# A transformer block on one core: first layer norm applied to a host-turned copy of the input, its moments spread over partitions through DRAM

## The reference, cut to what matters

```python
B, L, C = 32, 256, 288; H = 16; D = 18; FF = 1152; EPS = 1e-6
def _layernorm(x):
    mu = mean(x, -1); var = mean((x - mu)**2, -1)
    return (x - mu) * rsqrt(var + EPS)
ada = silu(c) @ W_ada + b_ada
shift_msa, scale_msa, gate_msa, shift_mlp, scale_mlp, gate_mlp = split(ada, 6)
h = _layernorm(x) * (1 + scale_msa) + shift_msa
x = x + gate_msa * attention(h, W_qkv, b_qkv, W_proj, b_proj)   # 16 heads of 18 channels
h = _layernorm(x) * (1 + scale_mlp) + shift_mlp
x = x + gate_mlp * (gelu(h @ W_fc1 + b_fc1) @ W_fc2 + b_fc2)
```

## Time and profile before

| what | value |
|---|---|
| median of 3 runs | 1234.8 us |
| the profiled execution's own time | 1228.32 us |
| span of its profile | 1226.5 us |
| PE, TensorE matmuls | 1181.1 us busy (96%), 9863 instructions |
| DVE, VectorE | 901.8 us (74%) |
| ACT, ScalarE | 866.1 us (71%) |
| POOL, GpSimd | 540.3 us (44%) |
| DMA | 188.91 MB, queue q1 busy 48.3% of 16 engines |

### The profile page before, as it was taken

The page is one execution under the profiler, slowest core; times in us unless marked ns, Lnnn a source line. Parts: engine busy times, 40 slices in busy tenths (PEclk is TensorE's granted clock), DMA queues, the critical chain, the costliest instruction groups (busy, mean ns, idle before and its releaser), DMA issues.

```text
span 1226.5 us, 27564 instructions
## 1 busy us (share of the span) xinstructions
PE 1181.1 (96%) x9863; PEld 1064.3 (87%) x9863; DVE 901.8 (74%) x1928; ACT 866.1 (71%) x1485; POOL 540.3 (44%) x557
## 2 busy tenths in 40 slices
PE   6888999999999999999999999999999999999977
PEld 5666999999998999999999999999999999997777
DVE  5687777877777787778777777777777787775553
ACT  5387777777777777777777777777777777778721
POOL 3012544444454444445454444444444445443364
PEclk9799999999999999999999999999999999999999
DMA  8554555554555554445555444555554555444220
GB/s 265 171 169 138 167 167 164 164 154 144 163 160 159 168 166 145 157 157 162 167 166 164 147 159 150 166 165 167 161 153 148 158 166 159 162 149 140 87 68 20
DMA packets 134330, 188.91 MB, mean 154 GB/s; under 512 B 24544, under 2 KB 102422, under 8 KB 133947
## 3 DMA queue, kind: packets, MB, share of 16 engines
q1 hardware_dynamic: 134033, 186.71, 48.3%
q10 hardware_dynamic: 162, 0.44, 0.1%
HBM read 121.92 MB, written 64.63 MB: 152 GB/s over the span
## 4 chain that ended last, share of the span: by engine, by line
PE 84%; SPq 5%; DMA 4%; DVE 3%; ACT 2%; issue 1%; POOL 0%; ACTq 0%; POOLq 0%; DVEq 0%
PE a_bank L867 10%; PE x_bank L785 10%; PE score_bank L808 9%; PE turn_bank L834 9%; PE st_bank L822 9%; PE b_bank L867 8%; PE b_bank L881 6%; PE b_bank L882 5%; PE b_bank L883 5%; PE a_bank L848 4%; PE x_bank L793 4%; SPq L623 2%; DMA qk_rows<-qst 1%; DMA ql<-zeros 1%; PE x_bank L759 1%
## 5 line engine op out<-in xcount | busy, mean ns | idle before, releaser
L1138 DVE TENSOR_REDUCE mx<-score_bank 128x2 f32<-128x512 f32 x512 | 342.0, 687 | 95.8 <-PE score_bank L808 93.7
L953 ACT ACTIVATE e<-st_bank 128x1024 f32<-128x1024 f32 x256 | 262.4, 1025 | 125.8 <-PE st_bank L822 123.5
L1287 POOL TENSOR_TENSOR gl<-gl_raw,gh 128x512 fp32r<-128x512 f32 (+1 forms) x160 | 194.3, 1221 | 226.4 <-DVE gh L1203 226.4
L946 ACT CAST ql<-mxt 4x256 fp32r<-4x256 f32 x512 | 206.2, 403 | 7.4 <-DVE mxt L1147 0.6
L808 PEld LDWEIGHTS score_bank<-kl,ql 122*128 122x128 f32 x1024 | 146.9, 190 | 42.0 <-issue 24.4
L808 PE MATMUL score_bank<-kl,ql 122*128 122x256 f32 x1024 | 174.6, 293 | 5.6 <-DMA ql<-zeros 3.3
L881 PE MATMUL b_bank<-w,gh 128*128 128x288 f32 x576 | 174.5, 303 | 2.2 <-DVE tmp L1209 1.9
L822 PE MATMUL st_bank<-ql,kl 122*128 122x512 f32 x512 | 165.7, 405 | 7.7 <-ACT e L953 6.9
L882 PE MATMUL b_bank<-w,gh 128*128 128x288 f32 x576 | 170.5, 296 | 0.0
L883 PE MATMUL b_bank<-w,gl 128*128 128x288 f32 x576 | 170.3, 296 | 0.0
L834 PE MATMUL turn_bank<-e,ve 128*32 128x256 f32 x2048 | 123.8, 382 | 0.3 <-ACT e L953 0.3
(11 more groups left out here) (152 smaller groups left out, 2473.1 us busy)
## 6 DMA issues: line engine op xcount, KB each, us to landing
qk_rows<-qst SPq DMA_DIRECT2D x128, 256.0 KB, 5.3
ql<-qk_rows SPq DMA_DIRECT2D x384, 72.0 KB
kl<-qk_rows SPq DMA_DIRECT2D x378, 72.0 KB
o_rows<-on SPq DMA_DIRECT2D x128, 128.0 KB
gate<-gates SPq DMA_DIRECT2D x32, 432.0 KB, 4.4
xin<-in_x SPq DMA_DIRECT2D x32, 288.0 KB, 5.9
x<-in_x SPq DMA_DIRECT2D x32, 288.0 KB, 3.0
out<-x SPq DMA_DIRECT2D x32, 288.0 KB, 4.5
```

The costliest lines, as they stand in the source:

```text
L946: last = nc.scalar.copy(rows[:, :, :, t, a, :], src)
L953: nc.scalar.activation(e[:, j % 4, :, :, :].rearrange("p u i l -> p (u i l)"), st_bank[:, :, :, :].rearrange("p u i l -> p (u i l)"), ACT. ...
L1138: nc.vector.tensor_reduce(mx[:, j // HP, i, :, col:col + 1], score_bank[i][:, :].rearrange("p (t l) -> p t l", t=NT), AX.X, ALU.max).then_ ...
L1287: nc.gpsimd.tensor_tensor(gl[:, cols], g[:, cols], gh[:, cols].bitcast(F32), ALU.subtract).then_inc(g_lo, 1)
```

## The change

The host hands over a second copy of x, `x_turned`, with channels on the partitions: per sample [128, 3, 256], the third block being the last 32 channels four times. The normalisation is made on that copy. For this the mean and the reciprocal deviation of every token must be present on every partition: VectorE and GpSimd put them in `mr1` (128 partitions x 2 tokens x 2 numbers), a DMA writes them to DRAM (`m_rows`, 2 KB a sample), and a second DMA reads these 2 KB back to all 128 partitions (`mrow`). Two `tensor_tensor` instructions over 128x768 then subtract the mean and multiply by the reciprocal deviation, in place in `xt_in`. ACT reads `xt_in` where it read `x_bank`. PE's `xt` is gone. `xin` has one buffer instead of two.

All five orders are written anew, head and tail too; the steps are those of before without PE's `xt`, and with `xc`, `mw`, `mr` on SyncE and `mod1` on POOL. In the head, ScalarE issues the first sample's `m_rows` write and read, x[0] is fetched ahead of the conditioning weights, and the conditioning products `mod` stand ahead of the first `s`.

```diff
 PE_ORDER = [
+    ("st", 0, 0), ("fc1", -3, 4), ("s", 0, 5), ("v", 1, 1), ("fc2", -3, 0), ("proj", -2, 0), ("s", 0, 6),
+    ("st", 0, 1), ("fc2", -3, 1), ("proj", -2, 1), ("st", 0, 2), ("s", 0, 7), ("fc2", -3, 2), ("st", 0, 3),
+    ("qk", 2, 0), ("fc2", -3, 3), ("s", 1, 0), ("pv", 0, 0), ("fc2", -3, 4), ("st", 0, 4), ("s", 1, 1),
...
 SYNC_ORDER = [
+    ("rr", -2, 0), ("qkr", 0, 10), ("qkr", 0, 11), ("qkr", 0, 12), ("or", -2, 0), ("or", -2, 1), ("xc", 2, 0),
...
+    ("rr", -2, 3), ("qkr", 0, 21), ("mw", 2, 0), ("qkw", 1, 0), ("sr", -1, 0), ("qkr", 0, 22), ("qkr", 0, 23),
+    ("or", -2, 5), ("qkr", 0, 24), ("qkr", 0, 25), ("mr", 2, 0), ("qkw", 1, 1), ("ln1_stats", 3, 0), ("rr", -2, 4),
...
 PE_HEAD = [
+    ("qk", 0, 0), ("qk", 0, 1), ("qk", 0, 2), ("gate5", 0, 0), ("v", 0, 0), ("gate2", 0, 0), ("v", 0, 1),
+    ("gate5", 0, 1), ("mod", 0, 0), ("s", 0, 0), ("gate5", 0, 2), ("s", 0, 1), ("gate2", 0, 1), ("gate2", 0, 2),
+    ("s", 0, 2), ("qk", 1, 0), ("s", 0, 3), ("qk", 1, 1), ("s", 0, 4), ("qk", 1, 2), ("s", 0, 5), ("st", 0, 0),
...
 ACT_HEAD = [
+    ("xt", 0, 0), ("xt", 0, 1), ("round", 0, 0), ("round", 0, 1), ("qk", 0, 0), ("qk", 0, 1), ("round", 0, 2),
+    ("qk", 0, 2), ("v", 0, 0), ("qkr", 0, 0), ("qkr", 0, 1), ("qkr", 0, 2), ("qkr", 0, 3), ("qkr", 0, 4),
+    ("qkr", 0, 5), ("round", 0, 3), ("round", 0, 4), ("round", 0, 5), ("round", 0, 6), ("v", 0, 1), ("xt", 1, 0),
...
@@ dit_block
-        xin = sb("xin", [P, 2, NT, C])
-        xn = sb("xn", [P, NT, CX])
+        xin = sb("xin", [P, NT, C])
+        xt_in = sb("xt_in", [P, 3, L])
+        mrow = sb("mrow", [P, L, 2])
+        mr1 = sb("mr1", [P, NT, 2])
...
+        def m_places(b):
+            return m_dram[b % 2].rearrange("(t p) s -> p t s", p=P), mr1[:, :, :]
+        def m_spread(b):
+            return (mrow[:, :, :].rearrange("p l s -> p (l s)"),
+                    m_dram[b % 2].rearrange("l s -> (l s)").unsqueeze(0).broadcast_to([P, 2 * L]))
@@ sync
+            def fetch_x(b):
+                wait(sp, ln1_dve, LN1 * (b - 1) + 1)
+                sp.dma_start(xin[:, :, :], x[b].rearrange("(p t) c -> p t c", t=NT)).then_inc(x_loaded, 16)
+            def fetch_columns(b):
+                wait(sp, x1_mod, 2 * b)
+                sp.dma_start(xt_in[:, :, :], x_turned[b]).then_inc(xt_loaded, 16)
+            def store_m(b):
+                sp.wait_ge(rstd1, b + 1)
+                if b >= 2:
+                    sp.wait_ge(m_rows, 16 * (b - 1))
+                sp.dma_start(*m_places(b)).then_inc(m_stored, 16)
+            def spread_m(b):
+                sp.wait_ge(m_stored, 16 * (b + 1))
+                wait(sp, ln1_dve, LN1 * b)
+                sp.dma_start(*m_spread(b)).then_inc(m_rows, 16)
             sp.dma_start(c_in, cond).then_inc(c_loaded, 16)
+            fetch_x(0)
...
@@ tensor
-            def xt(b, n):
-                pe.wait_ge(ln1_dve, 4 * b + 4)
-                wait(pe, x_drained, X_USES * b + n)
-                turn_x(x_bank, xn, n).then_inc(x_full, 1)
@@ scalar
+            act.wait_ge(rstd1, 1)
+            nc.scalar.dma_start(*m_places(0)).then_inc(m_stored, 16)
+            round_weights(0)
+            act.wait_ge(m_stored, 16)
+            nc.scalar.dma_start(*m_spread(0)).then_inc(m_rows, 16)
...
-                act.wait_ge(x_full, X_USES * b + n + 1)
+                act.wait_ge(ln1_dve, LN1 * (b + 1))
-                    last = nc.scalar.activation(v1[0:rows, c, :], x_bank[0:rows, (c % 2) * L:(c % 2 + 1) * L],
+                    last = nc.scalar.activation(v1[0:rows, c, :], xt_in[0:rows, c, :],
@@ vector
+            def ln1_moments(b):
+...
+                wait(dve, m_stored, 16 * b)
+                nc.vector.tensor_tensor(mr1[:, :, :], mv1[:, :, :], eps1[:, :, :], ALU.add).then_inc(ln1_dve, 1)
...
             def ln1_apply(b, t):
-                    normalise(xin[:, b % 2], mv1, rs1, xn, ln1_dve, rstd1, b, t)
+                if t == 0:
+                    dve.wait_ge(xt_loaded, 16 * (b + 1))
+                    dve.wait_ge(m_rows, 16 * (b + 1))
+                else:
+                    dve.wait_ge(ln1_dve, LN1 * b + 4)
+                row = mrow[:, :, t].unsqueeze(1).broadcast_to([P, 3, L])
+                nc.vector.tensor_tensor(xt_in[:, :, :], xt_in[:, :, :], row, (ALU.subtract, ALU.mult)[t]
+                                        ).then_inc(ln1_dve, 1)
@@ gpsimd
-                nc.gpsimd.tensor_tensor(rs1[:, :], ve1[:, :], mhalf[:, :], ALU.pow).then_inc(rstd1, 1)
+                nc.gpsimd.tensor_tensor(mr1[:, :, 1], mr1[:, :, 1], mhalf[:, :], ALU.pow).then_inc(rstd1, 1)
```

More of the change, by code:

```diff
@@ L50 @@
 OREM = 64 + 3 * D + 1
-X_USES = 2 + QK_PARTS + NT
-USE_QK, USE_V = 2, 2 + QK_PARTS
+LN1 = 5
+X_USES = QK_PARTS + NT
+USE_QK, USE_V = 0, QK_PARTS
 A_USES = NT + 2 + 3
@@ L101 @@
+    ("store", -4, 0), ("rr", -2, 5), ("qkw", 1, 2), ("ow", -1, 0), ("ow", -1, 1), ("qkw", 1, 3), ("sw", -1, 0),
+    ("qkw", 1, 4), ("res", -2, 0), ("qkr", 1, 0), ("qkr", 1, 1), ("qkr", 1, 2), ("qkr", 1, 3), ("qkr", 1, 4),
+    ("qkr", 1, 5),
 ]
 PE_HEAD = [
[14 rows of a table removed]
[13 rows of a table added]
 ]
 ACT_HEAD = [
-    ("xt", 0, 0), ("xt", 0, 1), ("round", 0, 0), ("round", 0, 1), ("qk", 0, 0), ("qk", 0, 1), ("qk", 0, 2),
-    ("round", 0, 2), ("round", 0, 3), ("round", 0, 4), ("v", 0, 0), ("round", 0, 5), ("qkr", 0, 0), ("qkr", 0, 1),
@@ new lines @@
+    ("qk", 0, 1), ("qk", 0, 2), ("split", 0, 0), ("ln1_stats", 1, 0), ("split", 0, 1), ("mod", 0, 0), ("max", 0, 0),
+    ("max", 0, 1), ("ln1_apply", 1, 0), ("ln1_apply", 1, 1), ("max", 0, 2), ("max", 0, 3), ("xt", 1, 0),
+    ("xt", 1, 1), ("ln1_stats", 2, 0), ("gates", 0, 0), ("max", 0, 4), ("split", 0, 2), ("max", 0, 5), ("qk", 1, 0),
+    ("max", 0, 6), ("max", 0, 7), ("mt", 0, 0), ("qk", 1, 1), ("max", 0, 8), ("max", 0, 9), ("max", 0, 10),
+    ("max", 0, 11), ("qk", 1, 2), ("ln1_apply", 2, 0), ("ln1_apply", 2, 1), ("max", 0, 12), ("ln1_stats", 3, 0),
@@ new lines @@
+    ("qkw", -1, 3), ("store", -6, 0), ("qkr", -1, 0), ("qkr", -1, 1), ("rr", -4, 4), ("qkr", -1, 2), ("qkr", -1, 3),
+    ("rr", -4, 5), ("qkr", -1, 4), ("qkr", -1, 5), ("qkr", -1, 6), ("qkw", -1, 4), ("res", -4, 0), ("qkr", -1, 7),
+    ("sw", -3, 0), ("qkr", -1, 8), ("sr", -3, 1), ("ow", -3, 2), ("qkr", -1, 9), ("qkr", -1, 10), ("ow", -3, 3),
+    ("qkr", -1, 11), ("qkr", -1, 12), ("or", -3, 0), ("qkr", -1, 13), ("qkr", -1, 14), ("qkr", -1, 15),
+    ("qkr", -1, 16), ("or", -3, 1), ("sw", -3, 1), ("qkr", -1, 17), ("qkr", -1, 18), ("rr", -3, 0), ("qkr", -1, 19),
@@ L270 @@
+    ("qkr", -1, 20), ("sr", -2, 0), ("qkr", -1, 21), ("qkr", -1, 22), ("ow", -2, 0), ("qkr", -1, 23),
[8 rows of a table added]
+    ("store", -1, 0),
 ]
@@ L399, in dit_block @@
         gates_stored = sem("gates_stored")
-        x_loaded = sems("x_loaded", 2)
+        x_loaded = sem("x_loaded")
+        xt_loaded = sem("xt_loaded")
+        m_stored = sem("m_stored")
+        m_rows = sem("m_rows")
+        x1_mod = sem("x1_mod")
         ln1_dve = sem("ln1_dve")
@@ L568, in load_weights, with x_columns, m_write, m_read @@
                                  w[k * P:(k + 3) * P, :].rearrange("(f p) c -> p f c", p=P)).then_inc(w_loaded[i], 16)
-            def fetch_x(b):
-                wait(sp, ln1_dve, 4 * b - 4)
-                sp.dma_start(xin[:, b % 2], x[b].rearrange("(p t) c -> p t c", t=NT)).then_inc(x_loaded[b % 2], 16)
             def ln1_stats(b, _):
-                if b >= 2:
+                if b:
                     fetch_x(b)
+            def x_columns(b, _):
+                if b:
+                    fetch_columns(b)
+            def m_write(b, _):
+                if b:
+                    store_m(b)
+            def m_read(b, _):
+                if b:
+                    spread_m(b)
             def res(b, _):
@@ L774, in qk @@
                 pe.wait_ge(x1_hi, 2 * b + 1)
-                pe.wait_ge(x_drained, X_USES * b + USE_QK + (n if b else n // 2))
+                wait(pe, x_drained, X_USES * b + USE_QK + (n if b else n // 2))
                 tiles, _rows, _ps = qk_tiles(b, n)
@@ L907, in _ @@
                                      ).then_inc(rows_cleared, 1)
-            for i in range(N_FIRST):
+            act.wait_ge(rstd1, 1)
[3 more added lines that the diff above has]
+            nc.scalar.dma_start(*m_spread(0)).then_inc(m_rows, 16)
+            for i in range(1, N_FIRST):
                 round_weights(i)
@@ L916, in xt @@
                     wait(act, x1_rem, b)
-                act.wait_ge(x_full, X_USES * b + n + 1)
+                    wait(act, x_full, X_USES * b)
+                act.wait_ge(ln1_dve, LN1 * (b + 1))
                 for c in (0, 1) if n == 0 else (2,):
                     rows = P if c < 2 else KR
-                    last = nc.scalar.activation(v1[0:rows, c, :], x_bank[0:rows, (c % 2) * L:(c % 2 + 1) * L],
+                    last = nc.scalar.activation(v1[0:rows, c, :], xt_in[0:rows, c, :],
```

(25 more changed lines are left out.)

165 lines of the change are left out of this document (74 added, 91 removed), and 181 rows, old and new, of tables (ACT_HEAD, ACT_ORDER, ACT_TAIL, DVE_HEAD).

## The result

The changed kernel takes 1306.7 us (median of 4 runs, 1301.1 to 1311.5) against 1234.1 us for the kernel before on the same chip. The ratio is 1.059, with an interval of 1.054 to 1.064. I had predicted 1215 us. The profiled execution took 1311.5 us at a span of 1309.7.

A forecast was written before the change was run, and what follows sets the result against it. PE was taken to bound the dense middle, with a period of 35.63 us. Removed turns (-18.1 us) and the head (-2) sum to -20.1, so from the median 1234.8 about 1215 us, range 1206 to 1234.

The forecast's parts named there:

- Both signs of being wrong: Profile checks: wrong if the PE period is 35.4 us or more; wrong in the head if equal PE work stands later at 144 us.
- the queue may be held 1 to 2 us, out of 6 us of room: SyncE's queue: the moments' read waiting for the write's landing holds it 1 to 2 us, absorbed by 6 us of room.
- Rival 3: Slower: SyncE's queue holds up the zero read of each first half, PE waiting on `ql<-zeros`; 1253 us, 13% chance.
- seven issues, some 3 us: SyncE's queue: seven issues, some 3 us, lie between the moments' write `mw` and read `mr`.
- Covered by the other 0.42: DMA: 11% more bytes, share from 0.52 to about 0.58, covered by the rest; landings perhaps some tenths later.
- 0.67 us a sample: PE: removing the turns of x saves 0.67 us a sample, 18.1 us over samples 5 to 31.
- My 0.17 for switching from turns to products: PE: part of the saving per sample, 0.09 and 0.08 us extra in the product groups following the turns.
- Rival 5: PE: turns go but the 0.17 us of switching stays, 4.6 us less gain; 1220 us, inside the forecast, no separate chance.
- The rival of 0.272 us a turn: PE: a turn takes 272 to 278 ns as its record reads, 44 us less in all; 1190 us, 1% chance.
- The two moment DMAs land by 13 to 17: Head: sample 0's moment transfers land by 13 to 17 us and decide the first q/k product only at their upper end.
- My bounds for the head, -7 to +5: Head: 2 us taken off in all, with -7 and +5 us as bounds.
- I had it fall from 27.75 to 26.6 us in 36: VectorE: busy time falls from 27.75 to about 26.6 us, copies gone and two applies added, covered by PE's 35.

The follow-up runs named there:

- number 4: Changed kernel without the write and read of the moments for samples 1 to 31 (part of the computation missing): 1232.3 us, ratio 0.999.
- number 6: As number 5, with the spreading read of samples 1 to 31 cut from 128 partitions (256 KB) to one (2 KB): 1242.0 us, ratio 1.007.
- number 5: Changed kernel with both moment transfers in place, but the read spreads sample 0's row without waiting for the write: 1250.8 us, ratio 1.015.
- number 1: Changed kernel with GpSimd's power and SyncE's write of the moments moved earlier for samples 7 to 31: 1256.4 us, ratio 1.019.
- number 9: Changed kernel with only GpSimd's power of the moments moved earlier from sample 7 on, SyncE's order kept: 1295.0 us, ratio 1.049.
- number 7: As number 4, with six turns a sample of the identity, read by nobody, put back on PE for samples 1 to 31: 1239.6 us, ratio 1.005.
- number 8: As number 1, with weight loads held until sample 0's moments landed and ScalarE's spreading read before its first cast: 1258.5 us, ratio 1.020.
- number 10: As number 1, with sample 0 normalised on VectorE and turned on PE, and sample 1's columns fetched at the start: 1242.5 us, ratio 1.008.

## Why the prediction was wrong

**The sum as the runs give it**, in ratios times 1234: without the spreading the change is worth -1 us (number 4), the two transfers with a tiny read +10 (number 6), the bytes of the read +9 (number 5), and the wait in SyncE's queue +55 (the changed kernel): 73 together. The -1 is itself a sum: in the profiles (number 4's is 3 us longer than that of the kernel before, which lay 6 under its median) the head loses 13 us and the middle gains 11. Both signs of being wrong that I had named came: a period over 35.4 (37.88), and later work at 144 us (sample 4's first scores 27 us later).

**The step that failed** is the one on SyncE's queue: "the queue may be held 1 to 2 us, out of 6 us of room". The hold was 2.24 us, near my size. The room was not where I had put it. I had counted room as time in which the queue issues nothing, 35 less 29 us. But the queue stands still because it waits for data, and in the kernel before the largest part of that is one wait at one place, `or` for PE's projection (total us, times, longest):

```profile
SPq L682 <- PE a_bank L848: 97.2, 28, 4.3
```

In the changed order that place comes after the `ow` writes, and the new wait stands ahead of them: the wait for PE shrank to 16.0 us, 18 times, but that came too late for `ow`. The chain is: SyncE stands at `mr`, `ow` goes late, ScalarE's copy of the attention output waits for its landing, the v copy behind it is late, and PE waits at the second v product. Removing the wait at its source gave back 50 to 56 us (numbers 1 and 5), and the hold on ScalarE and the time move together:

| kernel | SyncE waits for the write's landing, us | ScalarE's `on` copy held ("issue"), us | time, us |
|---|---|---|---|
| changed | 62.8 | 92.4 | 1306.7 |
| 9, power early | 51.5 | 84.0 | 1295.0 |
| 1, write early | 7.2 | 46.6 | 1256.4 |
| 5, read without wait | none listed | 44.7 | 1250.8 |
| 6, and a tiny read | none listed | 11.5 | 1242.0 |
| 4, no spreading | none | 5.5 | 1232.3 |

I had named q/k writes, x, two reads (they are of the reciprocal sums, `rr`) and the output behind the wait. The `ow` writes stand among them, and I neither listed them nor asked who waits for them. By the semaphore records ScalarE's copy stood for their landing 126.2 us in the changed kernel, 118.4 in number 9, 81.0 in number 1, 79.1 in number 5, 39.2 in number 6, 20.2 in number 4 and 9.6 in the kernel before.

**Rival 3** had the right queue and the wrong place and size. PE's wait on `ql<-zeros` did rise, from 3.3 us to 15.4, but the decisive wait is on the v copy.

**The write's place.** I took it that seven issues, some 3 us, between `mw` and `mr` would hide most of the landing. The write took 6.1 us to land in the median, so over 2 stayed.

**DMA.** "Covered by the other 0.42": the 256 KB of the read cost 9 us against a tiny one, with the DMA share of the middle at 0.56 to 0.64. The share of busy time said nothing about it.

**The turns.** 0.67 us a sample was too much: 0.36 by number 7; the orders with neither turns nor spreading run 0.47 under the old period. My 0.17 for switching from turns to products was the doubtful part of it; taking only the gaps that the turns themselves filled, 0.36 + 0.14 = 0.50, would have been nearer. Rival 5 (1220) was this case. The rival of 0.272 us a turn is excluded: it would make 1.6 us a sample. So would the Trainium skill's figure of about 275 ns a turn ("TensorE: Matmul & The Clock Gate", Part 4), if it is taken as a price and not as the latency of one.

**The head.** "The two moment DMAs land by 13 to 17": they landed at 18.6 and 25.7. I had taken landing times of a quiet stretch for a stretch with DMA at 0.85. With the loads held back the write landed in 3.3 us (number 8), and without sample 0's detour the kernel is 14 us faster (number 10). My bounds for the head, -7 to +5, didn't hold this. About 13 us more in the head, visible in sample 1, stay unexplained.

**VectorE.** The new instructions took what I had said (978 ns an apply, forecast 940 to 1060). The balance was wrong: I had it fall from 27.75 to 26.6 us in 36, and it rose to 29.98. Instructions that the change leaves alone took longer at their new places: `xr`, 32x256, took 459 ns on average before and 1322 after. In both traces it takes 417 ns with GpSimd all but idle beside it; with GpSimd at work through over half of it, it takes 1366 in the changed kernel, and such are 61 of 64 there and 5 of 64 before. It was covered: PE waits 2.6 us in all for the maxima.

No complete version tried beats the kernel before; the best is number 10 at 1.008. The one without spreading, which computes something else, only equals it: 0.47 us a sample gained in the middle pays just for the later start.

## What to carry to other kernels

A wait inside an in-order DMA queue is priced by who needs the transfers behind it, not by the idle share of the queue. Put the producer's write as many issues ahead of the dependent read as its landing takes, and do the same on the engine that makes the data. And for the first sample of a pipeline, a round trip through DRAM competes with the weight loads: a direct way for that sample alone was worth 14 us here.

## What had not been expected of the hardware

A write of 2 KB took 3.3 us to land with the weight loads held back (number 8) and 9.9 us behind them (number 1; 10.6 in the changed kernel), issued at the same time (7.95 and 7.96 us). From 200 to 1100 us of the changed kernel the two transfers are (issues of DMA: count, KB each, median us to landing):

```profile
mrow<-m_rows SPq DMA_DIRECT2D x23, 256.0 KB, 3.9
...
m_rows<-mr SPq DMA_DIRECT2D x23, 2.0 KB, 6.1
```

At these places the write of 2 KB, in pieces of 8 bytes, takes longer to land than the read of 256 KB. And a read of 256 KB a sample moved the period of a kernel whose DMA engines were 40% idle, from a nearly constant 35.17 us to between 35.16 and 36.60 (number 5), while the same two issues with 2 KB left it so (number 6). And a VectorE instruction of 417 ns took three times as long beside a working GpSimd.
